# Two residual layers on one core: three loads asked for in another order, adapter products of the short tiles a product later, and GpSimd's sums at the switch of halves held back

## The reference

```python
# layer 0: weight quantised to 8 levels with a low-rank delta
lora_delta = lora_B @ lora_A * 0.5
wg = (weight + lora_delta).reshape(O, I // 128, 128)
normalized = wg / exp(scale_log)
quantized = cb[searchsorted((cb[:-1] + cb[1:]) * 0.5, normalized)]
w_eff = (quantized * exp(scale_log)).reshape(O, I) + lora_delta
x = x + x @ w_eff.T
# layer 1: gated MLP, F = 2752, each with an adapter of rank 16 chosen per sample
gate = x @ W_gate.T + (x @ A_gate[i].T) @ B_gate[i].T * 0.5
up   = x @ W_up.T   + (x @ A_up[i].T)   @ B_up[i].T   * 0.5
act  = silu(gate) * up
x = x + act @ W_down.T + (act @ A_down[i].T) @ B_down[i].T * 0.5
```

## Time and profile before

| what | us |
|---|---|
| three runs | 1597.06, 1597.08, 1601.3 |
| median | 1597.08 |
| the profiled execution, its own time | 1595.55 |
| its span | 1593.9 |
| TensorE busy | 1567.1 (98%) |
| VectorE busy | 1237.8 (78%) |
| ScalarE busy | 566.3 (36%) |
| GpSimd busy | 533.1 (33%) |

### The profile page before, as it was taken

One profiled execution on the slowest core, in us unless ns is written; L12 is line 12 of the kernel. 1 busy time (PEld: TensorE's weight loads), 2 busy tenths in 40 slices (PEclk: granted clock), 3 DMA queues, 4 the chain that ended last, 5 costly groups with the idle time before them and its releaser, 6 DMA issues.

```text
span 1593.9 us, 21113 instructions
## 1 busy us (share of the span) xinstructions
PE 1567.1 (98%) x6968; PEld 1290.0 (81%) x6968; DVE 1237.8 (78%) x1575; ACT 566.3 (36%) x1006; POOL 533.1 (33%) x401
## 2 busy tenths in 40 slices
PE   7999999999999999998999999999999999999999
PEld 5878887778888888886888888888888888888887
DVE  7998969888888999998767887887676576795443
ACT  6411136333333333355333333333343233233231
POOL 4410013655545655625344555555310000000000
PEclk9999999999999999999999999999999999999999
DMA  9552175678878988872435666664378677676563
GB/s 304 124 109 76 50 233 124 183 212 215 229 198 223 238 223 217 240 275 79 119 119 145 184 175 180 173 173 144 104 204 216 162 172 196 158 215 208 156 184 120
DMA packets 368460, 281.25 MB, mean 176 GB/s; under 512 B 225120, under 2 KB 266848, under 8 KB 368224
## 3 DMA queue, kind: packets, MB, share of 16 engines
q1 hardware_dynamic: 246976, 240.77, 52.4%
q10 hardware_dynamic: 119296, 33.33, 8.9%
q0 software_dynamic: 2080, 5.80, 1.8%
HBM read 166.27 MB, written 110.85 MB: 174 GB/s over the span
## 4 chain that ended last, share of the span: by engine, by line
PE 86%; DVE 9%; DMA 2%; issue 2%; ACTq 1%; SPq 1%; ACT 0%; DVEq 0%
PE bank L1838 20%; PE bankA L1838 14%; PE bankC L1838 13%; PE bank L2076 10%; PE bankC L2076 7%; PE bankA L2076 6%; PE bankT L1985 3%; PE bank L1985 3%; PE bankT L2076 3%; DVE xl L1342 2%; PE bankT L1889 1%; PE bankT L1890 1%; PE bankC L1854 1%; DVE qsum L1634 1%; DVE rl L1333 1%
## 5 line engine op out<-in xcount | busy, mean ns | idle before, releaser
L991 ACT CAST rh<-wt 128x512 fp32r<-128x512 f32 x253 | 155.2, 620 | 383.8 <-PE bank L1838 87.0
L1333 DVE TENSOR_TENSOR rl<-wt,rh 128x512 fp32r<-128x512 f32 x253 | 239.9, 956 | 36.0 <-ACT rh L991 35.9
L1502 DVE TENSOR_TENSOR opl<-opl,oph 128x512 fp32r<-128x512 f32 (+1 forms) x154 | 107.8, 701 | 155.3 <-ACT oph L1128 155.0
L1838 PE MATMUL bank<-xh,rh 128*128 128x512 f32 x528 | 205.8, 390 | 0.2 <-DVE rl L1333 0.2
L1838 PE MATMUL bank<-xl,rh 128*128 128x512 f32 x528 | 205.6, 389 | 0.0
L1838 PE MATMUL bank<-xh,rl 128*128 128x512 f32 x528 | 205.5, 389 | 0.0
L1128 ACT CAST oph<-opl 128x512 fp32r<-128x512 f32 (+1 forms) x154 | 95.5, 621 | 268.7 <-DMA opl<-LT_d 263.6
L1838 PE MATMUL bankA<-xh,rh 128*128 128x512 f32 x352 | 137.9, 392 | 0.0
L1838 PE MATMUL bankA<-xl,rh 128*128 128x512 f32 x352 | 137.9, 392 | 0.0
L1838 PE MATMUL bankA<-xh,rl 128*128 128x512 f32 x352 | 137.7, 391 | 0.0
L1838 PE MATMUL bankC<-xh,rh 128*128 128x512 f32 x352 | 137.1, 389 | 0.0
(11 more groups left out here) (209 smaller groups left out, 3659.9 us busy)
## 6 DMA issues: line engine op xcount, KB each, us to landing
opl<-LT_d SPq DMA_DIRECT2D x148, 256.0 KB, 2.9
WT_d<-wt SPq DMA_DIRECT2D x88, 256.0 KB, 3.2
RT_d<-dt SPq DMA_DIRECT2D x70, 256.0 KB, 3.3
opl<-RT_d SPq DMA_DIRECT2D x70, 256.0 KB, 4.0
LT_d<-ev ACTq DMA_DIRECT2D x60, 256.0 KB, 2.6
wb<-WT_d SPq DMA_DIRECT2D x44, 256.0 KB, 3.4
wt<-WT_d SPq DMA_DIRECT2D x44, 256.0 KB, 3.4
dn<-in_L_cond_W_down_dram SPq DMA_DIRECT2D x86, 128.0 KB, 3.9
```

What stands on the lines that cost most here:

```text
L991: nc.scalar.copy(rh[:, v % RING, 0:KH * rows], wsrc(mm, RSRC[p])).then_inc(s_hi, 1)
L1333: dv.tensor_tensor(rl[:, v % RING, 0:KH * rows], wsrc(mm, RSRC[p]), rh[:, v % RING, 0:KH * rows].bitcast(f32), ALU.subtract).then_inc(s_lo, 1)
L1502: dv.tensor_tensor(opl[0:rows, L_AT[n % NL], :], opl[0:rows, L_AT[n % NL], :].bitcast(f32), oph[0:rows, L_AT[n % NL], :].bitcast(f32), ALU ...
L1838: last = te.matmul(OUT[p], a[:, u % RING, cols], b[:, OPND[p], k, :], start=k == 0 and n == 0, stop=k == KH - 1 and n == 2 and (p in (0, 1 ...
```

## The change

It has three parts.

In the head SyncE asks for the second weight block ahead of the token blocks 4 and 5, and for the third lora_B block ahead of token block 7.

At the short tiles the first pair of adapter products moves from u = 8 to 9 and the second from 10 to 11. In the tile after a short one `td` moves from steps 6, 8, 10 to 7, 9, 11; in the short tile of the switch its second moves from 8 to 9, and the low part for it on VectorE from 5 to 7.

At the switch GpSimd's first two activation sums move from step 4 to 5, behind the third weight sum, and wait until VectorE's second scaled row is done (`s_tlo` 6); its weight sums for the second half of the short tile wait for the first scaled row (`s_tlo` 5) in place of the low parts of x.

```diff
-        RIDE = {8: 0, 14: 1}
-        LATE = {10: 0, 16: 1}
+        RIDE = {9: 0, 14: 1}
+        LATE = {11: 0, 16: 1}
...
                 load_lb(1)
                 load_nat(2)
                 load_nat(3)
+                sp.wait_ge(s_dq, 2)
+                load_weight(1)
                 load_nat(4)
                 load_nat(5)
-                sp.wait_ge(s_dq, 2)
-                load_weight(1)
                 load_nat(6)
-                load_nat(7)
                 sp.wait_ge(s_trL, 2)
                 load_lb(2)
+                load_nat(7)
...
-                    turn = (5, 5, 7, 7) if first(it - 1) else (4, 4, 6, 6) if it == NJ else (1, 1, 3, 4)
+                    turn = (5, 5, 7, 7) if first(it - 1) else (5, 5, 6, 6) if it == NJ else (1, 1, 3, 4)
...
                     if 7 * m + p == turn[0] and after:
+                        if it == NJ:
+                            gp.wait_ge(s_tlo, 4 + 2)
                         act_sum(it - 1, 0)
                         act_sum(it - 1, 1)
                     if p == 2 and 0 <= mm + 1 < NM:
-                        if mm in (0, NH):
-                            gp.wait_ge(s_xlo, 14 + mm // NH * 14)
+                        if mm == 0:
+                            gp.wait_ge(s_xlo, 14)
+                        if mm == NH:
+                            gp.wait_ge(s_tlo, 4 + 1)
                         w_s12(mm + 1)
...
-                    dve_tail(u, (6, 8, 10) if first(it - 1) else (5, 9, 10) if it == NJ else (1, 4, 7))
+                    dve_tail(u, (6, 8, 10) if first(it - 1) else (7, 9, 10) if it == NJ else (1, 4, 7))
...
-                    td_at(u, (6, 8, 10, 12) if first(it - 1) else (3, 8, 10, 12) if it == NJ else (0, 3, 6, 9))
+                    td_at(u, (7, 9, 11, 12) if first(it - 1) else (3, 9, 11, 12) if it == NJ else (0, 3, 6, 9))
```

## The result

The changed kernel took 1603.28 us as the median of 20 runs (1597.34 to 1608.64), the kernel before 1598.24 us beside it (20 runs, 1596.87 to 1604.15). The ratio is 1.0021, 95% interval 1.0013 to 1.0030, which is 3.4 us; the two medians are 5.0 us apart, the two means 3.5. Timed again on another chip the ratio was 1.0028 (1.0012 to 1.0045). The forecast was 1592.5 us with 1587.0 to 1597.8: wrong in sign, and the time lies outside the range. The profiled execution of the changed kernel took 1600.31 us, span 1598.7, against 1595.55 and 1593.9.

The account below looks back on a forecast made before the run. TensorE, busy 98% of 1593.9 us, was taken as the bound, with some 27 us of standing to win. Head -2.4, first short tile and next -0.2, switch -2.0 made -4.6: 1597.08 to 1592.5 us, range 1587.0 to 1597.8.

Parts of the forecast that it names:

- td, -0.9 or 0: Tile after the first short one: activation product's 0.90 us stand goes with td a product later; -0.9 taken, 0 if lateness travels.
- First short tile, +0.7 for RIDE and LATE: First short tile: the 1.83 us stand goes, but the late add comes three pieces, 2.2 us, later; +0.7 us net.
- the first rival: Whole kernel: the stalls simply go, -9.0 us, 1588.1 us, of which the half clock could lose 2.1 again; chance 0.20.
- its own case: The forecast itself, -4.6 us over head, short tiles and switch, own range -3 to -6.5 us; chance 0.47.
- Switch, -2.0: Switch of halves, 717 to 745 us: all moves there together give 3.0 to 1.2 us; -2.0 taken, bounds -8.0 and +5.1.
- Head, -2.4: Head: less data ahead of lora_B's third-block rows removes TensorE's whole 2.41 us stall; -2.4 us, bounds -2.4 and +1.5.
- The price, the fifth token block: Head: fifth token block has half a megabyte more ahead of it, 1.5 us; used only as the upper bound.
- The fourth, slower: Switch: sums held back on GpSimd delay VectorE's late add, with half clock on top; +4.9 us overall, 1602.0 us; chance 0.08.

Follow-up runs that it names:

- e2: The kernel before with the tables RIDE (8 to 9) and LATE (10 to 11) changed alone: ratio 1.0004.
- R: The part that moves the tables RIDE (8 to 9) and LATE (10 to 11); alone against the kernel before: ratio 1.0004.
- e3: The changed kernel with td in the tile behind each short one put back to 6, 8, 10, 12: ratio 1.0020 to the kernel before.
- e18: The changed kernel with ScalarE's rounding and VectorE's low parts moved along with td behind each short tile: ratio 1.0011 to the kernel before.
- e19: The changed kernel timed once more, on the same chip as GpSimd's hold-back alone: 1602.06 us, ratio 1.0028 to the kernel before.
- e15: The kernel before with the head's order, RIDE 9, LATE 11 and GpSimd's hold-back; td and low parts at the switch as before: ratio 1.0013.
- e6: The kernel before with only td a product later in the tile behind each short one (7, 9, 11, 12): ratio 1.0029.
- G with S: The kernel before with GpSimd's hold-back and, in the tile at the switch, td and VectorE's low parts moved: ratio 0.9989.
- H with R: The kernel before with the head's new request order and RIDE 9, LATE 11: ratio 0.9994.
- G: The kernel before with GpSimd's hold-back at the switch alone: ratio 0.9987, timed again 0.9990.
- e8: The changed kernel without GpSimd's hold-back: ratio 1.0031 to the kernel before.
- H: The part that changes the order of SyncE's requests in the head; alone against the kernel before: ratio 1.0002.

## Why the prediction was wrong, by its own steps

- **td, -0.9 or 0: the step that failed first.** The prediction asked only whether the low part would be there in time. It did not ask who waits for td. The bound had no side above zero; alone the edit costs 4.4 us by the medians of the timed runs (ratio 1.0029), of which the profile shows 2.4. The order of before had td and the rounding in the same steps (6, 8, 10) for a reason that the code shows: `wait(act, s_tdm, n)` ahead of a single buffer.
- **First short tile, +0.7 for RIDE and LATE.** The late add behind three more pieces was right, its size was not, and the half clock was missing. The late add was to start three pieces, 2.2 us, later; it starts at 271.18, which against the 270.25 of the earlier trace rows and with the head's 2.06 us taken off is 3.0 later, because the take of the seventh product had moved into the same stretch. That makes +1.90 (e2) instead of +0.7. And the half clock behind the wait, 1.6 to 1.9 us, came in six of the eight profiles with R. The prediction had it in the first rival alone, and wrote for its own case that the late add covers it; in those six the half clock came right behind the new wait of 2.5 us that it forecast. The Trainium skill, "TensorE: Matmul & The Clock Gate", section "HAM oscillation — how this bites in real kernels", says that waits for data between short bursts of matmuls bring the half clock back; here a single wait of 2.7 to 3.2 us behind a long run of matmuls did so in those six, and in the other two (3.06 and 2.66 us) it did not.
- **Switch, -2.0.** The path was read well up to product 12, and the half clock behind it was not priced. The pair takes 0.89 us (0.9 forecast), the wait for a low part is 2.21 us at 727.48 (2.4), the third product begins 3.9 us earlier than before, counted from u = 160 (3.9), and product 12 begins 1.4 us earlier (3.0 to 1.2) behind a wait for the late add of 2.39 us. Then comes the second stretch at the half clock, 1.9 us by the chain and 1.7 by the starts of products, and leaves +0.34. In e3 and e18, whose late add waits as long without that stretch, the switch gives 1.28 and 1.30 us, inside the forecast's bounds. In e19 the stretch is missing as well, but TensorE waits 2.62 us for the activation's low part where it waited 1.14, and the switch gives only 0.31. That the hold-back alone gives 2.0 (2.01, 2.08) is no success of the forecast: its -2.0 was a middle value for all the moves at the switch. The terms do not add either: RIDE and LATE alone give 2.33 and the hold-back 2.01, both together (e15) 1.14, since the two parts fight for one stand.
- **Head, -2.4.** Right in the profile after (the wait gone, -2.06 at u = 0; the request of L1920 at 54.60 instead of 56.99) and wrong in the mean. The price, the fifth token block, was named and bounded at +1.5 us, from the bytes put ahead of it, and then left at nothing; nine of ten profiles pay it. The bytes were the smaller part: the block is asked for 3.8 us later, behind SyncE's wait for `s_dq`, which the sum did not have. Timed: 0.0002 of the whole.
- **The rivals.** The fourth, slower, had the right sign and nearly the right time (1602.0), with only half of the mechanism: the held-back sums do make the late add late, but only together with LATE 11, and it had no part for td. That its number fits is in good part luck.

What stays open: where e6 loses the rest of its 4.4 us, with 2.4 in its profile (the granted clocks point to the half clock), and why G with S (-1.8 by the ratio) and H with R (-1.0) make +3.2 together in e3. The late add at the switch (e15, +2.1 where H R and G alone would make -3.1) is the only part of it that a run shows.

## What to carry to other kernels

Before an instruction is moved later, ask who waits for it, not only what it waits for: the reader of a single buffer holds back whoever fills it, and an in-order list passes that on to everything behind. Where two edits aim at the same stand, do not add their gains; try each alone, since here the one that won (0.13%) was hidden under one that cost 0.29%. Before a transfer is asked for earlier, look at the wait that its request brings along: it now holds back every request behind it. A new wait of 2 to 3 us on TensorE should be priced with a chance of the half clock behind it, here 1.6 to 1.9 us more: six times in eight at the first short tile, once in six at the switch.

## What the runs showed of the hardware

The half clock behind a wait is no sure thing: the same wait in front of product 12 of the first tile was followed by a clock of 0.66 (2.98 us, changed kernel) and by one of 1.00 (3.06 us, e2; 2.66 us, e18). In front of product 12 of the switch the clock fell behind a wait of 2.39 us (changed kernel, 0.60) and not behind 2.36 (e3), 2.38 (e18) or 3.12 us (e15), nor behind the shorter ones of e19 (1.81) and e8 (1.52). The start of the first MLP product varies from 235.17 to 242.64 us over the twenty profiles, whatever stands behind it. All five that are more than 4 us late have a stretch at the 1.2 GHz level between 30 and 48 us, with H and without it, behind a wait for tokens or for lora_B; of the other fifteen, four have one too. Windows of e3 first, then of the changed kernel's first profile (columns as above):

```profile
33.00:36.00 3.00, 2.52 (x8) 0.50 1.08 352
36.00:39.00 3.00, 3.00 (x12) 0.50 0.77 274
```

```profile
33.00:36.00 3.00, 3.00 (x22) 1.00 1.08 350
36.00:39.00 3.00, 3.00 (x21) 1.00 1.04 256
```

In the same 6 us one execution did 20 instructions and the other 43. This spread of the head, 7.5 us, is larger than every effect measured here, so a single profile says what a part does inside its stretch, and only many timed runs say what it does to the whole.
